# A graph network kernel: four PSUM banks for messages and two for falls in layers 1 to 3

## The chip, the cores and the metric

The kernel runs on one core of a Trainium2 chip. The metric is the device time of one execution in microseconds, and the median of several runs counts. All times in this document are microseconds unless they are marked ns.

## The reference

A graph of 3125 nodes and 100000 edges, sorted by target node, goes through four layers. Each layer gathers, for each edge, the features of its source node, adds the edge's own features, and takes a softmax-weighted mean over the edges of each target node, feature by feature. Then each node's sum goes through a small network of two linear maps with a normalisation.

```python
def _genconv(h, edge_attr, src, dst, w1, b1, g1, bb1, w2, b2, t):
    msg = jax.nn.relu(h[src] + edge_attr) + EPS_MSG
    m = msg * t
    seg_max = jax.lax.stop_gradient(jax.ops.segment_max(m, dst, num_segments=N))
    ex = jnp.exp(m - seg_max[dst])
    denom = jax.ops.segment_sum(ex, dst, num_segments=N)
    alpha = ex / (denom[dst] + 1e-16)
    agg = jax.ops.segment_sum(msg * alpha, dst, num_segments=N)
    out = h + agg
    z = jax.nn.relu(_layernorm(out @ w1 + b1, g1, bb1))
    return z @ w2 + b2
...
h = x @ enc_node_w + enc_node_b
e = edge_attr @ enc_edge_w + enc_edge_b
h = _genconv(h, e, src, dst, ...)                      # layer 0
for i in range(1, L):                                  # layers 1 to 3
    z = jax.nn.relu(_layernorm(h, ln_g[i], ln_b[i]))
    h = h + _genconv(z, e, src, dst, ...)
return jax.nn.relu(_layernorm(h, ln_g[0], ln_b[0]))
```

Before this x is normalised, and the result is added to x. There are 64 features.

## The kernel before

The edges are cut into two halves, which lie beside each other on the 128 partitions (64 features each). Each half is 98 chunks of 512 edges, so a tile is 128 x 512, which fills one PSUM bank of f32. A layer is a loop over the 98 chunks (the chunk phase), then a phase over the nodes. The five engines each run their own program in order, and semaphores tie them together; what is printed below as a loop over chunks is unrolled. Layer 0 is written out, and layers 1 to 3 are one loop.

For a chunk c of layers 1 to 3:

- GpSimd (POOL) issues 8 indirect DMAs (line L521) that gather 128 rows of `z_rows` each into `zsrc[c % 4]`. It waits for `x_mm` of chunk c - 4, which says that this buffer was read.
- TensorE (PE) writes the *falls* (L776): a tile that is 0 inside a run of edges of one target and -1e30 where a new target begins. Two matmuls. Then `add_edges` (L785), one matmul of the edge features by their weights, and `add_nodes` (L790), which transposes the gathered rows onto the same bank and signals `x_mm`.
- ScalarE (ACT) does `messages(c)`: relu to `r` (L599), times t to `u` (L601), times t back into the bank (L602).
- VectorE (DVE) does `running_max(c)`: a scan (L1100) over falls and `u` into `M`, then L1102, L1106 (the falls' bank becomes the exponent of the decay) and L1108 (the messages' bank becomes the exponent of the weight).
- ScalarE does `copy_out(c - 1)`, then `exps(c)`: the decay from the falls' bank to SBUF (L606), the exponential in the messages' bank (L608).
- VectorE does `running_sums(c)`: scan S (L1117), a product (L1119), scan W (L1121), which signals `sw_done`.
- TensorE does `back(c)`: eight transposes (L801) of S and W into the banks pT0 and pT1. ScalarE's `copy_out(c)` (L614, two of 512 columns) brings them to SBUF, and SyncE (SP) stores them to `sw_rows` (L388). SyncE's queue also loads the edge features, six pairs of chunks ahead (L380).

When all chunks are stored, GpSimd fetches the 25 groups of rows that end the nodes' runs (L532), and the node phase begins. Its result, `z_rows`, is what GpSimd waits for before the next layer's first gather. In between, the seam of the two halves is mended (L1232 to L1254).

TensorE's program sets the order of the work around the change. For chunk c it is `back(c - 3)`, `falls(c)`, `add_edges(c)`, `add_nodes(c)`, and behind the last chunk the three transposes that are left. The falls and the messages take their banks in turn from three each, so both wait for the chunk c - 3: the falls for `decay_done`, the edges for `sw_done`. VectorE's scan L1100 waits for `u_done` alone; since the falls of a chunk stand ahead of its additions, they are ready when `u` is. `banks` and `done(...)` turn a chunk into a semaphore's value (`PRE` = 2 is added to each at the start).

## Time and profile before

| | us |
|---|---|
| median of 3 runs | 4319.33 |
| lowest, highest | 4317.49, 4326.74 |
| the profiled execution | 4317.04 |
| its span | 4315.2 |

| engine | busy us | share of the span |
|---|---|---|
| GpSimd (POOL) | 3058.1 | 71% |
| VectorE (DVE) | 2874.9 | 67% |
| TensorE (PE) | 2470.6 | 57% |
| ScalarE (ACT) | 1759.0 | 41% |

The span runs from the first to the last instruction; 1.8 us of the profiled execution's time lie around it. Busy time leaves out register, branch, semaphore and DMA-issuing instructions of the engines, but a gather that GpSimd issues is shown as a span on GpSimd. "Issue" is idle time of an engine that waits for nothing that the profile shows. In the timeline, the bracket behind a row is the idle time of its engine before it, and what ended it. The mean granted clock of TensorE is 0.678 of full speed.

### The profile page before, as it was taken

Reading aid. Unit: us, or ns where it says so; the run is one execution under the profiler, and the core shown is the slowest. Engines: PE = TensorE matmul, PEld = TensorE weight load, DVE = VectorE, ACT = ScalarE, POOL = GpSimd, SP = SyncE. Lnnn points to the kernel's source line nnn. Section 1 sums busy time; section 2 is a strip of 40 time slices with the busy share of each in tenths; the row PEclk is TensorE's granted clock in tenths of the full one; section 3 lists DMA queues with packets and bytes.
Section 4 is the critical chain, followed back from the end, with each engine's and each line's share of the span. In section 5 each row is a group of like instructions: output and inputs, shape, how many; then the busy total and the mean of one; then the engine's idle time right before and its main releaser. Section 6 shows DMA issues by size and latency. Waiting matters only on the chain.

```text
span 4315.2 us, 37180 instructions
## 1 busy us (share of the span) xinstructions
PE 2470.6 (57%) x9731; PEld 1778.7 (41%) x9731; DVE 2874.9 (67%) x3973; ACT 1759.0 (41%) x3487; POOL 3058.1 (71%) x3248
## 2 busy tenths in 40 slices
PE   4666776665555555555555555555555555555554
PEld 3555555543433333333433333333343333333333
DVE  5888888875566666666656666666664666666665
ACT  2444444444433443334334433444343334443344
POOL 3777777775577777777557777777746777777773
PEclk9776667666566666666557666666656667666765
DMA  3545554554233333333223333333323333333332
GB/s 86 148 142 146 148 142 142 147 146 139 65 105 105 109 104 104 105 105 109 77 72 109 105 101 108 105 109 105 101 70 87 102 108 105 109 105 101 108 105 64
DMA packets 307125, 469.66 MB, mean 109 GB/s; under 512 B 169424, under 2 KB 175306, under 8 KB 306893
## 3 DMA queue, kind: packets, MB, share of 16 engines
q1 hardware_dynamic: 200286, 356.83, 24.0%
q0 software_dynamic: 103552, 109.52, 12.6%
q8 instruction: 86, 1.41, 0.1%
q14 instruction: 147, 1.20, 0.1%
q10 hardware_dynamic: 3054, 0.71, 0.1%
HBM read 217.93 MB, written 248.86 MB: 108 GB/s over the span
## 4 chain that ended last, share of the span: by engine, by line
POOL 69%; issue 23%; PE 2%; DVE 2%; DMA 1%; ACT 1%; POOLq 0%; ACTq 0%; DVEq 0%; SPq 0%
POOL zsrc L521 68%; POOL node_sw L532 1%; DMA zsrc<-z_rows,idx_all 1%; PE pT L801 0%; PE pR L898 0%; PE pX L790 0%; DMA node_sw<-sw_rows,row_idx 0%; PE pX L723 0%; PE pX L879 0%; DVE z L1295 0%; DMA sw_rows<-sw_out 0%; ACT sq L654 0%; ACT sw_out L614 0%; POOLq L517 0%; DMA z_rows<-z 0%
## 5 line engine op out<-in xcount | busy, mean ns | idle before, releaser
L521 POOL DMA_INDIRECT zsrc<-z_rows,idx_all x3136 | 2960.4, 944 | 1089.2 <-issue 979.3
L790 PE MATMUL pX<-ident,zsrc 128*128 128x128 f32 x2368 | 591.8, 429 | 1207.0 <-DMA zsrc<-z_rows,idx_all 1206.8
L614 ACT ACTIVATE sw_out<-pT 128x512 f32<-128x512 f32 x784 | 425.3, 594 | 1822.9 <-PE pT L801 1821.2
L790 PEld LDWEIGHTS pX<-ident,zsrc 128*128 128x128 f32 x2368 | 505.6, 316 | 1521.6 <-DMA zsrc<-z_rows,idx_all 1521.6
L1117 DVE TENSOR_TENSOR_SCAN S<-decay,S,pX 128x512 f32<-128x512 f32 x296 | 378.1, 1277 | 691.2 <-ACT decay L606 688.5
L801 PE MATMUL pT<-ident,S 128*128 128x128 f32 x1568 | 630.4, 406 | 46.2 <-DVE W L1121 46.2
L801 PE MATMUL pT<-ident,W 128*128 128x128 f32 x1568 | 619.3, 400 | 0.0
L1100 DVE TENSOR_TENSOR_SCAN M<-pR,M,u 128x512 f32<-128x512 f32 x296 | 376.8, 1273 | 235.1 <-ACT u L601 235.1
L785 PE MATMUL pX<-attr_pair,edge_w 128*128 128x512 f32 x592 | 435.4, 825 | 12.6 <-ACT attr_pair L593 12.5
L790 PE MATMUL pA<-ident,zsrc 128*128 128x128 f32 x768 | 195.0, 434 | 426.8 <-DMA zsrc<-z_rows,idx_all 426.8
L599 ACT ACTIVATE r<-pX,edge_b 128x512 f32<-128x512 f32 x296 | 204.7, 692 | 494.8 <-PE pX L790 494.8
L1121 DVE TENSOR_TENSOR_SCAN W<-decay,W,pX 128x512 f32<-128x512 f32 x296 | 378.9, 1280 | 10.4
L790 PEld LDWEIGHTS pA<-ident,zsrc 128*128 128x128 f32 x768 | 166.8, 321 | 527.4 <-DMA zsrc<-z_rows,idx_all 527.4
L801 PEld LDWEIGHTS pT<-ident,S 128*128 128x128 f32 x1568 | 358.4, 229 | 49.4 <-issue 36.4
L801 PEld LDWEIGHTS pT<-ident,W 128*128 128x128 f32 x1568 | 356.3, 227 | 0.0
L1117 DVE TENSOR_TENSOR_SCAN S<-decay,S,pA 128x512 f32<-128x512 f32 x96 | 122.9, 1280 | 320.7 <-ACT decay L606 320.7
L601 ACT ACTIVATE u<-r,t_now 128x512 f32<-128x512 f32 x392 | 283.0, 722 | 12.8
L1102 DVE TENSOR_TENSOR pR<-pR,M 128x512 f32<-128x512 f32 x296 | 207.0, 699 | 10.2
L1119 DVE TENSOR_TENSOR pX<-r,pX 128x512 f32<-128x512 f32 x296 | 205.9, 696 | 10.2
L1106 DVE TENSOR_TENSOR pR<-pR,M 128x512 f32<-128x512 f32 x296 | 207.0, 699 | 3.4
L1108 DVE TENSOR_TENSOR pX<-pX,M 128x512 f32<-128x512 f32 x296 | 203.9, 689 | 0.0
L602 ACT ACTIVATE pX<-r,t_now 128x512 f32<-128x512 f32 x296 | 199.0, 672 | 0.0
(201 smaller groups left out, 3130.9 us busy)
## 6 DMA issues: line engine op xcount, KB each, us to landing
sw_rows<-sw_out SPq DMA_DIRECT2D x392, 512.0 KB, 2.9
attr_pair<-attr_cols SPq DMA_DIRECT2D x153, 512.0 KB, 4.6
zsrc<-z_rows,idx_all POOLq DMA_INDIRECT x3136
attr_in<-in_edge_attr_dram SPq DMA_DIRECT2D x196, 128.0 KB
attr_cols<-attr_pair SPq DMA_DIRECT2D x49, 512.0 KB, 3.1
max_cols<-M SPq DMA_DIRECT2D x49, 256.0 KB, 3.1
z_rows<-z SPq DMA_DIRECT2D x25, 125.0 KB
node_sw<-sw_rows,row_idx POOLq DMA_INDIRECT x100, 2.5
```

The lines of the kernel that those rows point to most:

```text
L521: pool.indirect_dma_start(zsrc[c % RING][:, t4, h, :], None, z_rows, bass.IndirectOffsetOnAxis(idx_all[:, h, t4, c:c + 1].bitcast(U32), 0) ...
L601: act.activation(u[s][:, :], r[s][:, :], ACT.Copy, scale=t_now[:, 0:1]).then_inc(u_done, 1)
L614: act.activation(sw_out[c % 2][:, :, 2 * b:2 * b + 2, :, :].rearrange("p h t s c -> p (t s) h c"), pT[b][:, :].rearrange("p (a h c) -> p a ...
L785: pe.matmul(messages_bank(c, first_layer)[:, :], edge_w2[:, :], attr_t(c), start=True, stop=False, skip_group_check=True)
L790: last = pe.matmul(messages_bank(c, first_layer)[:, t4:CH:SUB], zsrc[c % RING][:, t4, :, :].rearrange("p h c -> p (h c)"), ident[:, :], st ...
L801: last = pe.transpose(pT[b][:, at:at + P], scanned[c % 2][:, t4:CH:SUB], ident[:, :])
L1100: v.tensor_tensor_scan(m[:, at + 1:at + CH + 1], falls[:, :], u[c % 2][:, :], m_last, ALU.add, ALU.max).then_inc(m_done, 1)
L1102: v.tensor_tensor(falls[:, :], falls[:, :], m[:, at:at + CH], ALU.add).then_inc(d_done, 1)
L1106: v.tensor_tensor(falls[:, :], falls[:, :], m[:, at + 1:at + CH + 1], ALU.subtract).then_inc(dm_done, 1)
L1117: v.tensor_tensor_scan(S[s][:, :], decay[s][:, :], msg[:, :], S[s1][:, CH - 1:CH], ALU.mult, ALU.add).then_inc(s_done, 1)
L1119: v.tensor_tensor(msg[:, :], r[s][:, :], msg[:, :], ALU.mult).then_inc(rex_done, 1)
L1121: v.tensor_tensor_scan(W[s][:, :], decay[s][:, :], msg[:, :], W[s1][:, CH - 1:CH], ALU.mult, ALU.add).then_inc(sw_done, 1)
```

## The change

In layers 1 to 3 the bank pH goes over from the falls to the messages. Messages then take four banks in turn (pX0, pX1, pA, pH), falls two (pR0, pR1), as in layer 0. The edges of chunk c wait for `sw_done` of chunk c - 4, the falls for `decay_done` of chunk c - 2. TensorE's program for chunk c becomes `back(c - 4)`, `add_edges(c)`, `add_nodes(c)`, `falls(c - 2)`, and behind the last chunk stand `back` and `falls` of what is left. Since the falls no longer stand ahead of their chunk's additions, they have a semaphore of their own, `falls_mm`, and VectorE's scan waits for it in all layers.

```diff
--- before.py
+++ after.py
@@ -232,11 +232,10 @@
 
         def messages_bank(c, first_layer):
 
-            return pX[c % 2] if first_layer else (pX + [pA])[c % 3]
-
-        def falls_bank(c, first_layer):
-
-            return pR[c % 2] if first_layer else (pR + [pH])[c % 3]
+            return pX[c % 2] if first_layer else (pX + [pA, pH])[c % 4]
+
+        def falls_bank(c):
+            return pR[c % 2]
 
         par_in = sem("par_in")
         dst_in = sem("dst_in")
@@ -264,6 +263,7 @@
         attr_tp = sem("attr_tp")
         attr_sb = sem("attr_sb")
         x_mm = sem("x_mm")
+        falls_mm = sem("falls_mm")
         r_done = sem("r_done")
         u_done = sem("u_done")
         u_ps_done = sem("u_ps_done")
@@ -603,7 +603,7 @@
 
                 def exps(c):
                     act.wait_ge(dm_done, done(g0 + c))
-                    act.activation(decay[c % 2][:, :], falls_bank(c, first_layer)[:, :], ACT.Exp).then_inc(decay_done, 1)
+                    act.activation(decay[c % 2][:, :], falls_bank(c)[:, :], ACT.Exp).then_inc(decay_done, 1)
                     act.wait_ge(um_done, done(g0 + c))
                     act.activation(messages_bank(c, first_layer)[:, :], messages_bank(c, first_layer)[:, :], ACT.Exp).then_inc(ex_done, 1)
 
@@ -738,6 +738,7 @@
 
             pe.sem_inc(attr_tp, PRE)
             pe.sem_inc(x_mm, PRE)
+            pe.sem_inc(falls_mm, PRE)
             pe.sem_inc(back_tp, PRE)
             pe.sem_inc(node_tp, PRE)
             pe.sem_inc(y_mm, PRE)
@@ -760,7 +761,7 @@
                     pe.wait_ge(z_ready, l * NG)
                     pe.sem_inc(pe_passed, 1)
 
-                banks = 2 if first_layer else 3
+                banks = 2 if first_layer else 4
 
                 def attr_to_channels(c):
                     pe.wait_ge(attr_loaded[c % 2], 32 * (c // 2 + 1))
@@ -771,10 +772,11 @@
                     last.then_inc(attr_tp, 1)
 
                 def falls(c):
-                    pe.wait_ge(decay_done, done(g0 + (c - banks)))
+                    pe.wait_ge(decay_done, done(g0 + (c - 2)))
                     for h in range(2):
-                        pe.matmul(falls_bank(c, first_layer)[h * H:(h + 1) * H, :], chunk_sel[:, c:c + 1].to_broadcast([NCH, H]), fall_sb[:, h, :],
-                                  start=True, stop=True)
+                        last = pe.matmul(falls_bank(c)[h * H:(h + 1) * H, :], chunk_sel[:, c:c + 1].to_broadcast([NCH, H]), fall_sb[:, h, :],
+                                         start=True, stop=True)
+                    last.then_inc(falls_mm, 1)
 
                 def add_edges(c):
                     if first_layer:
@@ -813,9 +815,9 @@
                 if first_layer:
                     attr_to_channels(0)
                     pe.matmul(pH[0:NP, 0:NK], zeros_b[:, :], zeros_b[:, 0:NK], start=True, stop=False, **hist_mm)
-                falls(0)
-                add_edges(0)
                 if first_layer:
+                    falls(0)
+                    add_edges(0)
                     for c in range(NCH):
                         add_nodes(c)
                         if c + 1 < NCH:
@@ -841,18 +843,18 @@
                             falls(c + 1)
                             add_edges(c + 1)
                 else:
-                    add_nodes(0)
-                    for c in range(1, 3):
-                        falls(c)
+
+                    for c in range(NCH):
+                        if c >= 4:
+                            back(c - 4)
                         add_edges(c)
                         add_nodes(c)
-                    for c in range(3, NCH):
-                        back(c - 3)
+                        if c >= 2:
+                            falls(c - 2)
+                    for c in range(NCH - 2, NCH):
+                        back(c - 2)
                         falls(c)
-                        add_edges(c)
-                        add_nodes(c)
-                    for c in range(NCH - 3, NCH - 1):
-                        back(c)
+                    back(NCH - 2)
                 back(NCH - 1)
 
                 pe.wait_ge(seam_mean, l + 1)
@@ -1086,7 +1088,7 @@
 
                 def running_max(c):
                     q, at = c // 2, (c % 2) * CH
-                    falls, msg, m = falls_bank(c, first_layer), messages_bank(c, first_layer), M[q % 2]
+                    falls, msg, m = falls_bank(c), messages_bank(c, first_layer), M[q % 2]
                     if at == 0:
                         m_last = M[(q - 1) % 2][:, 2 * CH:2 * CH + 1]
                         v.tensor_copy(m[:, 0:1], m_last)
@@ -1096,6 +1098,7 @@
                             dve.wait_ge(m_stored[q], 16 * (M_STORES[q] + 1))
                     else:
                         m_last = m[:, at:at + 1]
+                    dve.wait_ge(falls_mm, done(g0 + c))
                     dve.wait_ge(u_done, done(g0 + c))
                     v.tensor_tensor_scan(m[:, at + 1:at + CH + 1], falls[:, :], u[c % 2][:, :], m_last, ALU.add, ALU.max).then_inc(m_done, 1)
                     dve.wait_ge(m_done, done(g0 + c))
```

TensorE's program at the end of the chunk phase, from the falls or edges of chunk 97 on, before (names as in the section on the kernel; L801 is `back`, whose eight transposes are cut to the first, pR1 and pX1 are the banks of chunk 97):

```order
L776 MATMUL pR1<-fall_sb,chunk_sel 64x512 [waits decay_done]
...
L785 MATMUL pX1<-attr_pair6,edge_w2 128x512 [waits sw_done,cols_loaded6]
L790 MATMUL pX1<-ident,zsrc1 128x128 [waits gathered1]
L790 MATMUL pX1<-ident,zsrc1 128x128 x3
...
L797 REGISTER_ALU [waits sw_done]
L801 MATMUL pT0<-ident,S1 128x128 [waits back_sb]
...
L797 REGISTER_ALU [waits sw_done]
L801 MATMUL pT0<-ident,S0 128x128 [waits back_sb]
...
L797 REGISTER_ALU [waits sw_done]
L801 MATMUL pT0<-ident,S1 128x128 [waits back_sb]
```

The same place after the change (L777 is the falls, L787 the edges, L792 the nodes, L803 `back`):

```order
L787 MATMUL pX1<-attr_pair6,edge_w2 128x512 [waits sw_done,cols_loaded6]
L792 MATMUL pX1<-ident,zsrc1 128x128 [waits gathered1]
L792 MATMUL pX1<-ident,zsrc1 128x128 x3
L777 MATMUL pR1<-fall_sb,chunk_sel 64x512 [waits decay_done]
L777 MATMUL pR1<-fall_sb,chunk_sel 64x512
...
L799 REGISTER_ALU [waits sw_done]
L803 MATMUL pT0<-ident,S0 128x128 [waits back_sb]
...
L777 MATMUL pR0<-fall_sb,chunk_sel 64x512 [waits decay_done]
...
L799 REGISTER_ALU [waits sw_done]
L803 MATMUL pT0<-ident,S1 128x128 [waits back_sb]
...
L777 MATMUL pR1<-fall_sb,chunk_sel 64x512 [waits decay_done]
```

Before, the falls of chunk 97 stand ahead of its additions and three transposes (S1, S0, S1: chunks 95, 96, 97) behind them. Now the falls of chunk 95 (pR1) follow the additions of chunk 97, then come the transposes of chunk 94, the falls of 96 (pR0), the transposes of 95, and the falls of 97 (pR1). The transposes of 96 and 97 follow and are not shown.

VectorE's program for one chunk of layers 1 to 3, before (the scans are named SCALAR_TENSOR_TENSOR here):

```order
L1100 SCALAR_TENSOR_TENSOR M1<-pH,M0,u0 128x512 [waits u_done]
L1102 TENSOR_TENSOR pH<-pH,M1 128x512 [waits m_done]
L1104 COPY kept_max<-M1 128x1
L1106 TENSOR_TENSOR pH<-pH,M1 128x512 [waits d_done]
L1108 TENSOR_TENSOR pA<-pA,M1 128x512 [waits u_ps_done]
L1117 SCALAR_TENSOR_TENSOR S0<-decay0,S1,pA 128x512 [waits sw_done,back_tp,ex_done,decay_done]
L1119 TENSOR_TENSOR pA<-r0,pA 128x512 [waits s_done]
L1121 SCALAR_TENSOR_TENSOR W0<-decay0,W1,pA 128x512 [waits rex_done]
```

And after:

```order
L1103 SCALAR_TENSOR_TENSOR M1<-pR0,M0,u0 128x512 [waits u_done,falls_mm]
L1105 TENSOR_TENSOR pR0<-pR0,M1 128x512 [waits m_done]
L1107 COPY kept_max<-M1 128x1
L1109 TENSOR_TENSOR pR0<-pR0,M1 128x512 [waits d_done]
L1111 TENSOR_TENSOR pA<-pA,M1 128x512 [waits u_ps_done]
L1120 SCALAR_TENSOR_TENSOR S0<-decay0,S1,pA 128x512 [waits sw_done,back_tp,ex_done,decay_done]
L1122 TENSOR_TENSOR pA<-r0,pA 128x512 [waits s_done]
L1124 SCALAR_TENSOR_TENSOR W0<-decay0,W1,pA 128x512 [waits rex_done]
```

The instructions and their order are the same on VectorE; the scan into M waits for `falls_mm` too, and banks have changed.

## Rows read from the trace of the kernel before

**Rows 1.** The page's part 4: shares of the chain that ended last.

```profile
POOL 69%; issue 23%; PE 2%; DVE 2%; DMA 1%; ACT 1%; POOLq 0%; ACTq 0%; DVEq 0%; SPq 0%
```

**Rows 2.** GpSimd's line L521, layers 1 to 3: durations, then idle us, times.

```profile
L521 POOL DMA_INDIRECT zsrc<-z_rows,idx_all x2352: 940/944/961, 1118.5 to 4222.6; - x196
...
  issue: 741.9, 2346
  DMA z_rows<-z: 53.0, 2
  PE pX L790: 0.9, 3
  PE pA L790: 0.3, 1
```

**Rows 3.** Timeline of GpSimd: start us, us, what, idle before.

```profile
1059.86 0.94 POOL L532 DMA_INDIRECT node_sw<-sw_rows,row_idx  x1 [23.17 <-DMA sw_rows<-sw_out]
...
1118.51 0.94 POOL L521 DMA_INDIRECT zsrc<-z_rows,idx_all  x1 [25.69 <-DMA z_rows<-z]
...
2095.90 0.96 POOL L521 DMA_INDIRECT zsrc<-z_rows,idx_all  x1 [0.30 <-issue]
...
2122.14 0.94 POOL L532 DMA_INDIRECT node_sw<-sw_rows,row_idx  x1 [25.28 <-DMA sw_rows<-sw_out]
...
2182.28 0.94 POOL L521 DMA_INDIRECT zsrc<-z_rows,idx_all  x1 [27.32 <-DMA z_rows<-z]
```

**Rows 4.** Waits, layers 1 to 3: us in total, times, longest.

```profile
POOL node_sw L532 <- DMA sw_rows<-sw_out: 75.4, 3, 25.3
```

**Rows 5.** Chain that ended last, drain of layer 1: start us, us, what.

```profile
2098.38 2.08 PE pX L790 x8
2100.45 1.72 PE pT L801 x8
...
2104.41 1.29 DVE S L1117
...
2106.45 1.29 DVE W L1121
...
2112.09 1.29 DVE S L1117
...
2117.63 1.09 ACT sw_out L614 x2
2118.74 2.61 DMA sw_rows<-sw_out
```

**Rows 6.** Timeline, all engines, before and in that drain.

```profile
2092.46 0.64 PE L776 MATMUL pR<-fall_sb,chunk_sel 98*64 98x512 bf16 x2
...
2093.03 1.26 PE L785 MATMUL pX<-attr_pair,edge_w 128*128 128x512 f32 x2
...
2098.07 1.27 DVE L1100 TENSOR_TENSOR_SCAN M<-pR,M,u 128x512 f32<-128x512 f32 x1
...
2100.03 0.23 PEld L801 LDWEIGHTS pT<-ident,S 128*128 128x128 f32 x1
...
2100.72 0.69 DVE L1108 TENSOR_TENSOR pX<-pX,M 128x512 f32<-128x512 f32 x1
...
2102.25 1.09 ACT L614 ACTIVATE sw_out<-pT 128x512 f32<-128x512 f32 x2 [5.64 <-PE pT L801]
...
2103.70 0.62 ACT L608 ACTIVATE pX<-pX 128x512 f32<-128x512 f32 x1
```

**Rows 7.** Timeline of TensorE: two node additions of layer 2, closest found.

```profile
2274.76 2.08 PE L790 MATMUL pA<-ident,zsrc 128*128 128x128 f32 x8 [6.10 <-DMA zsrc<-z_rows,idx_all]
...
2283.33 1.16 PE L790 MATMUL pX<-ident,zsrc 128*128 128x128 f32 x8 [3.74 <-DMA zsrc<-z_rows,idx_all]
```

**Rows 8.** Waits in layer 0, 200 to 1000 us.

```profile
DVE M L1100 <- ACT u L601: 137.0, 76, 3.6
```

**Rows 9.** Windows: engines busy us (instructions), TensorE's clock, DMA share, GB/s.

```profile
2100.00:2108.00 8.00, 2.29 (x12) 1.90 (x11) 4.93 (x8) 3.96 (x7) 0.00 (x0) 0.50 0.16 66
```

## Prediction

> **What bounds the kernel now.** I read the chain of waits first. On the page, 69% of the chain that ended last is GpSimd and 23% is "issue", GpSimd's own gap between two gathers [rows 1]. So of every edit I ask whether it reaches GpSimd. Next I read line L521 over layers 1 to 3, from their first gather to their last: 2352 gathers of 944 ns, and the idle time before them is 741.9 us "issue" (0.30 us each, and a loop start), 53.0 us for the z rows at two layer starts, and only 0.9 + 0.3 = 1.2 us for TensorE's node additions, which is the one thing that PSUM banks can influence [rows 2]. GpSimd is never short of a free gather buffer. A chunk takes 8 x 1.248 = 9.98 us of it, and 784 gathers take from 1118.51 to 2096.86, 978 us, whatever the other engines do [rows 3].
>
> What remains of a layer is 1063.8 us (from 1118.51 to 2182.28) less 978: about 85 us in which GpSimd waits. Of it, 25.28 us lie between the last gather and the first fetch of node sums [rows 3]; over three layers this wait is 75.4 us [rows 4]. This is the drain: the last chunks run through the other engines with nothing beside them. The chain of layer 1's drain shows each link [rows 5]: node additions of chunk 97 at 2098.38 (call it T), transposes L801 of chunk 95, copy L614, decay, scan S of chunk 96 at 2104.41 (T + 6.03), W, transposes, copy, S of chunk 97 at 2112.09, transposes, copy at 2117.63, the store, then GpSimd at 2122.14. One chunk of the drain costs 2112.09 - 2104.41 = 7.68 us. Note what is already running at T: the running maximum (L1100) of chunk 96 started at 2098.07, before T [rows 6].
>
> **The change part by part.**
>
> *Four message banks instead of three.* The addition of chunk c now waits for the sums of chunk c-4, not c-3. It can only let an addition go sooner, and additions wait for the gather, with TensorE idle 3.74 to 6.10 us before them [rows 7]. Value at most the 1.2 us of [rows 2] in the whole kernel; I take 0.
>
> *The transposes go back one chunk further.* TensorE did back(c-3) ahead of the additions of chunk c; now back(c-4). ScalarE stands at copy_out(c-1), behind which are exps(c) and messages(c+1), until back(c-1) is done, so all of ScalarE's work after it, and VectorE's sums, come one chunk later against the gathers. SyncE's store of the copied rows (with the load of edge columns queued behind it, which runs six pairs ahead) comes later too. None of these holds GpSimd: its condition is the addition of chunk c-4, and a chunk landed has some three laps, 30 us, to be added. In steady state this costs nothing.
>
> *The falls two chunks behind, with a signal.* falls(c-2) now stands behind the additions of chunk c, and VectorE's running maximum of chunk c-2 waits for it. Queued behind that wait is all of VectorE's work on the chunk; ScalarE's exps wait for it, then S and W, then the transposes. So from the falls to the end of W is the new lap: by VectorE, maximum to L1108's end 3.34 us (2098.07 to 2101.41, [rows 6]), exp to S 0.70 (2103.70 to 2104.41), S to W's end 3.32 (2104.41 to 2107.73), together 7.4; by the transposes behind the falls, to the copy 2.2, copy to S 2.16 (2102.25 to 2104.41), S to W 3.32, together 7.7. The lap available is 9.98 on average and 8.57 in the shortest that I found (2274.76 to 2283.33, [rows 7]). It fits, so again nothing in steady state. In layer 0 TensorE's order is unchanged and the falls are ready a chunk ahead; VectorE's additional wait is covered by 137.0 us of waiting for u over 76 chunks [rows 8]: 0.
>
> *The drain.* Here the cover is gone. At T VectorE used to be in the middle of chunk 96's maximum; now even chunk 95's has not begun, since falls(95) stand behind the additions of chunk 97. So three chunks have to pass instead of two, one of them half done. In steps, layer 1:
> - T to the first matmul behind the additions: unchanged, 1.65 us (2098.38 to 2100.03, [rows 6]).
> - falls(95), newly ahead of the transposes: 0.57 us (2092.46 to 2093.03, [rows 6]), up to 0.9 with the gap around them. I take 0.75.
> - back(94), copy, exps, S of chunk 95: as before for back(95) to S(96), so S(95) starts at T + 6.03 + 0.75 = T + 6.8. VectorE's own path is no later: falls ready at T + 2.4, maximum 3.34, exp 0.70, T + 6.5.
> - S(95) to S(96), S(96) to S(97): 7.68 each. falls(96) stand ahead of back(95) and wait for nothing late; falls(97) stand behind back(95), done some 3 us after W(95), and the maximum of chunk 97 is wanted only after W(96).
> - S(97) therefore at T + 6.8 + 15.4 = T + 22.1, before T + 13.7. Everything behind it (last transposes, store, fetch of node sums, seam) shifts as it is.
>
> Growth per layer 0.75 + 7.68 = 8.4 us, for three layers 25.3 us. The waits of the three drains are alike (75.4 over 3, longest 25.3), so one serves for all. T itself cannot come earlier: it is 1.5 us after GpSimd's last gather ends (2096.86 to 2098.38). Bounds per layer: below, if the two cycles ran at what VectorE is busy in one plus the exp (3.32 for the sums and 3.34 for the maximum are 6.66, plus 0.70: 7.36), 0.57 + 7.68 - 2 x 0.32 = 7.6; above, if each of three chunks lost another 0.7 to the later falls and additional waits, 10.5. So 23 to 32 us in three layers. I take 25.3, since the cycle of 7.68 us is one that the trace shows whole.
>
> Sum: 4317.04 + 25.3 = 4342.3 us against the profiled execution, which lies 2.3 us under the median of 4319.33. Against the median it is 4344.6; I forecast 4344.5.
>
> TensorE's granted clock is 0.50 (1.2 GHz) in the drain, where it is busy 2.29 of 8 us [rows 9]. The transposes' durations used here are read at this level, so a drain that is longer at the same level brings no further term.
>
> **Rivals.**
>
> *A. More banks pay, and the drain does not grow.* Place: GpSimd's wait for node additions, and the first step after T. Price: 1.2 us gained at most [rows 2], so about 4318 us. It needs a drain in which chunk 95 and 96 overlap so well that each layer grows by under 2.9 us (8.6 us in all, 0.2%); from there the result is no longer slower. For it: TensorE and ScalarE are mostly idle in the drain. Against it: VectorE is busy 6.66 of each 7.68 us there, and one more whole chunk must go through it after T. The Trainium skill speaks for this rival: its page "Perfetto Trace Analysis", section "Matmuls", says that independent matmul groups should rotate through different PSUM banks, so that reading one out overlaps the next group's matmuls. By this rule alone the kernel would gain. The trace does not bear it out here: what more overlap could still free is the 1.2 us of GpSimd's waits [rows 2].
>
> *B. The lagged lap does not fit.* If falls, maximum, exps, S and W, transposes and additions ran in series, a chunk would take 1.65 + 0.57 + 3.34 + 0.70 + 3.32 + 2.2 + 1.26 (additions of edges, [rows 6]) = 13.0 us. It decides from 9.98 us on: then TensorE falls behind, GpSimd finds its four buffers full, and the kernel becomes 3.0 x 98 x 3 = 880 us longer, 5200 in all. For it: three engines in one loop, where TensorE stands in order. Against it: 7.7 us by the rows, and the transposes wait for a W of the lap before.
>
> *C. The drain is hidden.* If the fetch of node sums waited for something else than the last store, the drain would cost nothing and the time stay at 4319. Against it: the wait is put down to the store in all of the three layers, and the chain runs through it [rows 4, 5].
>
> **How the numbers follow.** Forecast 89%; A 3%; B 3%; C 3%; 2% for a GpSimd or DMA effect of unknown sign. A difference under 0.2% (8.6 us) can't be told from no change in this kernel. The growth of 23 to 32 us on the median gives 4342 to 4351; with the runs' own spread of some 2 us I give 4339 to 4352. Faster by over 0.2%: 2% (1 of A, 1 unknown). Within: 5% (2 of A, 3 of C). Slower: 93% (89 + 3 of B + 1 unknown).
>
> **What would show it.** In the profile after: gathers from first to last of a layer still 978 us; GpSimd's wait ahead of the node fetch 33 to 34 us in layers 1 to 3 and unchanged (23.17, [rows 3]) in layer 0; three S scans of the last bank cycle behind the last gathered additions, 7.7 us apart, where there were two; no wait of GpSimd for additions. The forecast is wrong if that wait is under 28 us or the gathers of a layer take over 980 us.

## The result, and the profile after

The changed kernel takes 4346.95 us (median of 4 runs, 4346.4 to 4347.7), the kernel before 4318.9 us (median of 4 runs). The ratio of the two is 1.0066 (95% interval 1.0054 to 1.0077): slower by 28 us, inside the forecast range of 4339 to 4352, and 2.5 us over the forecast of 4344.5. The profiled execution took 4346.48 us (span 4344.7), 29.4 us more than that of before.

The page of the changed kernel, parts 1, 4 and 5 (columns as for before):

```profile
PE 2503.0 (58%) x9731; PEld 1769.0 (41%) x9731; DVE 2902.7 (67%) x3973; ACT 1769.2 (41%) x3487; POOL 3057.9 (70%) x3248
...
POOL 66%; issue 22%; DMA 4%; PE 4%; DVE 2%; ACT 1%; POOLq 0%; DVEq 0%; ACTq 0%; SPq 0%
...
L521 POOL DMA_INDIRECT zsrc<-z_rows,idx_all x3136 | 2960.4, 944 | 1089.8 <-issue 968.7
L1103 DVE TENSOR_TENSOR_SCAN M<-pR,M,u 128x512 f32<-128x512 f32 x392 | 503.3, 1284 | 1009.6 <-PE pR L777 829.0
```

GpSimd still leads the chain [rows 1], with the same 2960.4 us in the gathers. The large new wait is VectorE's, 829.0 us for the falls (L777). It is idle time of an engine that does not set the pace, so by its size it says nothing of the 28 us.

GpSimd's line L521 in layers 1 to 3 of the changed kernel, which answers to [rows 2]:

```profile
L521 POOL DMA_INDIRECT zsrc<-z_rows,idx_all x2352: 938/944/962, 1117.1 to 4242.2; - x196
its engine sat idle before it (us, times) until:
  issue: 731.3, 2310
  DMA z_rows<-z: 53.4, 2
  PE pX L792: 7.0, 23
  PE pH L792: 4.3, 14
  PE pA L792: 0.9, 3
```

The waits for additions have grown from 1.2 to 12.2 us, but "issue" has shrunk by as much: 731.3 + 12.2 = 743.5, before 741.9 + 1.2 = 743.1. The longest of these waits is 0.3 us: they are the same gaps of 0.30 us under another label. A layer's gathers take 978.3 to 978.4 us, as before.

GpSimd's timeline at the drains of layers 0 to 3 and its waits there, which answer to [rows 3, 4]:

```profile
1058.42 0.94 POOL L532 DMA_INDIRECT node_sw<-sw_rows,row_idx  x1 [21.82 <-DMA sw_rows<-sw_out]
...
2131.01 0.94 POOL L532 DMA_INDIRECT node_sw<-sw_rows,row_idx  x1 [35.52 <-DMA sw_rows<-sw_out]
...
3204.53 0.94 POOL L532 DMA_INDIRECT node_sw<-sw_rows,row_idx  x1 [35.06 <-DMA sw_rows<-sw_out]
...
4278.85 0.94 POOL L532 DMA_INDIRECT node_sw<-sw_rows,row_idx  x1 [35.69 <-DMA sw_rows<-sw_out]
```

```profile
POOL node_sw L532 <- DMA sw_rows<-sw_out: 106.3, 3, 35.7
```

The wait has grown from 75.4 to 106.3 us: 30.9 us. Layer 0 gave back 1.35 us (23.17 before, 21.82 now). 30.9 - 1.35 is 29.5, which is the whole difference of the spans. So the drains of layers 1 to 3 are the place; all else cancels. Layer 0's gain was not forecast, and no run explains it (s2 lies 1.6 us under s1 there as well, f1 0.4 us over the kernel before).

The chain in the drain of layer 1, which answers to [rows 5]:

```profile
2094.53 4.28 DMA zsrc<-z_rows,idx_all
2098.85 2.08 PE pX L792 x8
2100.93 0.57 PE pR L777 x2
2101.49 1.69 PE pT L803 x8
2103.27 1.08 ACT sw_out L614 x2
...
2105.59 1.29 DVE S L1120
...
2109.05 1.99 PE pT L803 x8
...
2113.28 1.29 DVE S L1120
...
2120.97 1.29 DVE S L1120
...
2126.50 1.09 ACT sw_out L614 x2
2127.61 2.61 DMA sw_rows<-sw_out
```

Three S scans stand behind the last additions (T = 2098.85) where there were two, 7.69 us apart. S of chunk 97 starts at T + 22.12. The forecast said T + 22.1. But T itself is late: GpSimd's last gather ended at 2131.01 - 35.52 = 2095.49, so T is 3.36 us behind it, and was 1.52 us behind. In layers 2 and 3 it is 2.82 and 3.46 (before 1.47 and 1.46). Split in two, the growth of the three waits is

| | layer 1 | layer 2 | layer 3 | sum |
|---|---|---|---|---|
| last gather's end to T, longer by | 1.84 | 1.35 | 2.00 | 5.2 |
| T to the fetch of node sums, longer by | 8.40 | 8.80 | 8.45 | 25.7 |

SyncE's queue shows what meets the last gather. Before:

```profile
2083.40 0.33 SPq L388 DMA_DIRECT2D sw_rows<-sw_out  x1
2083.84 0.37 SPq L380 DMA_DIRECT2D attr_pair<-attr_cols  x1
2093.74 0.33 SPq L388 DMA_DIRECT2D sw_rows<-sw_out  x1
```

After:

```profile
2092.82 0.33 SPq L388 DMA_DIRECT2D sw_rows<-sw_out  x1
...
2093.26 0.37 SPq L380 DMA_DIRECT2D attr_pair<-attr_cols  x1
```

The layer's last load of edge columns (L380, 512 KB) stands in SyncE's program behind a store that waits for ScalarE's copy. The copy comes one chunk later now, and with it the load moved from 2083.84 (13.0 us ahead of the last gather's end) to 2093.26, 2.2 us ahead of that end at 2095.49. In layers 2 and 3 it is the same: 13.0 and 12.9 us ahead before, 1.8 and 2.2 us after.

### The profile page after: what moved, and what is told of

Its sections match the earlier page's. It is cut to its first block, busy times and chain, and to the rows that moved or that the text cites. A ratio compares the mean times of both kernels' runs of the same rounds, so it can differ in the third digit from the quotient of the medians.

```text
span 4344.7 us, 37515 instructions
## 1 busy us (share of the span) xinstructions
PE 2503.0 (58%) x9731; PEld 1769.0 (41%) x9731; DVE 2902.7 (67%) x3973; ACT 1769.2 (41%) x3487; POOL 3057.9 (70%) x3248
## 3 DMA queue, kind: packets, MB, share of 16 engines
q1 hardware_dynamic: 200286, 356.83, 23.7%
## 4 chain that ended last, share of the span: by engine, by line
POOL 66%; issue 22%; DMA 4%; PE 4%; DVE 2%; ACT 1%; POOLq 0%; DVEq 0%; ACTq 0%; SPq 0%
POOL zsrc L521 65%; DMA zsrc<-z_rows,idx_all 3%; POOL node_sw L532 1%; PE pX L792 1%; PE pT L803 1%; PE pH L792 0%; PE pR L900 0%; ACT sw_out L614 0%; PE pX L881 0%; DVE S L1120 0%; DVE W L1124 0%; PE pX L723 0%; DMA node_sw<-sw_rows,row_idx 0%; ACT sq L654 0%; DVE z L1298 0%
## 5 line engine op out<-in xcount | busy, mean ns | idle before, releaser
L521 POOL DMA_INDIRECT zsrc<-z_rows,idx_all x3136 | 2960.4, 944 | 1089.8 <-issue 968.7
L1103 DVE TENSOR_TENSOR_SCAN M<-pR,M,u 128x512 f32<-128x512 f32 x392 | 503.3, 1284 | 1009.6 <-PE pR L777 829.0
L792 PE MATMUL pX<-ident,zsrc 128*128 128x128 f32 x1984 | 474.6, 414 | 964.8 <-DMA zsrc<-z_rows,idx_all 964.8
L792 PEld LDWEIGHTS pX<-ident,zsrc 128*128 128x128 f32 x1984 | 404.6, 302 | 1258.6 <-DMA zsrc<-z_rows,idx_all 1258.6
L803 PE MATMUL pT<-ident,S 128*128 128x128 f32 x1568 | 649.2, 418 | 68.3 <-DVE W L1124 67.8
L803 PE MATMUL pT<-ident,W 128*128 128x128 f32 x1568 | 618.4, 399 | 0.0
L803 PEld LDWEIGHTS pT<-ident,S 128*128 128x128 f32 x1568 | 348.9, 222 | 196.2 <-issue 183.8
L1120 DVE TENSOR_TENSOR_SCAN S<-decay,S,pX 128x512 f32<-128x512 f32 x248 | 316.8, 1278 | 129.0 <-ACT decay L606 126.4
L787 PE MATMUL pX<-attr_pair,edge_w 128*128 128x512 f32 x496 | 379.8, 859 | 23.1 <-ACT attr_pair L593 12.1
L792 PE MATMUL pH<-ident,zsrc 128*128 128x128 f32 x576 | 149.5, 441 | 394.9 <-DMA zsrc<-z_rows,idx_all 394.9
L599 ACT ACTIVATE r<-pX,edge_b 128x512 f32<-128x512 f32 x248 | 170.9, 689 | 478.1 <-PE pX L792 478.1
L803 PEld LDWEIGHTS pT<-ident,W 128*128 128x128 f32 x1568 | 352.8, 225 | 0.0
L792 PEld LDWEIGHTS pH<-ident,zsrc 128*128 128x128 f32 x576 | 128.3, 328 | 483.6 <-DMA zsrc<-z_rows,idx_all 483.6
L1124 DVE TENSOR_TENSOR_SCAN W<-decay,W,pX 128x512 f32<-128x512 f32 x248 | 317.5, 1280 | 8.7
L1105 DVE TENSOR_TENSOR pR<-pR,M 128x512 f32<-128x512 f32 x392 | 274.1, 699 | 13.6
L792 PE MATMUL pA<-ident,zsrc 128*128 128x128 f32 x576 | 137.2, 413 | 250.4 <-DMA zsrc<-z_rows,idx_all 250.4
L1109 DVE TENSOR_TENSOR pR<-pR,M 128x512 f32<-128x512 f32 x392 | 274.1, 699 | 3.4
L606 ACT ACTIVATE decay<-pR 128x512 f32<-128x512 f32 x392 | 236.3, 603 | 93.4 <-DVE pR L1109 91.0
L792 PEld LDWEIGHTS pA<-ident,zsrc 128*128 128x128 f32 x576 | 116.6, 300 | 329.2 <-DMA zsrc<-z_rows,idx_all 329.2
L777 PE MATMUL pR<-fall_sb,chunk_sel 98*64 98x512 bf16 x784 | 235.6, 599 | 0.0
```

Source lines behind the costliest of these rows:

```text
L521: pool.indirect_dma_start(zsrc[c % RING][:, t4, h, :], None, z_rows, bass.IndirectOffsetOnAxis(idx_all[:, h, t4, c:c + 1].bitcast(U32), 0) ...
L606: act.activation(decay[c % 2][:, :], falls_bank(c)[:, :], ACT.Exp).then_inc(decay_done, 1)
L787: pe.matmul(messages_bank(c, first_layer)[:, :], edge_w2[:, :], attr_t(c), start=True, stop=False, skip_group_check=True)
L792: last = pe.matmul(messages_bank(c, first_layer)[:, t4:CH:SUB], zsrc[c % RING][:, t4, :, :].rearrange("p h c -> p (h c)"), ident[:, :], st ...
L803: last = pe.transpose(pT[b][:, at:at + P], scanned[c % 2][:, t4:CH:SUB], ident[:, :])
L1103: v.tensor_tensor_scan(m[:, at + 1:at + CH + 1], falls[:, :], u[c % 2][:, :], m_last, ALU.add, ALU.max).then_inc(m_done, 1)
```

## The experiments

Most experiments met a second condition, in which the kernel before took 5037 to 5137 us where it took 4319 in the first comparison, while the engines' instructions had their usual lengths. One of these chips (the one of e5_zero_lag) gave 4318 us for the same kernel at a later time, so this is a condition and not a property of the chip. The expectations call it "late transfers". That name is a guess, and the trace of e5 speaks against it as the whole cause. ScalarE's relu (L599) waits there for TensorE's additions (L790) and a product of VectorE that is long done, for no transfer:

```profile
1704.37 1.52 PE L790 MATMUL pX<-ident,zsrc 128*128 128x128 f32 x8
...
1707.71 0.38 PE L801 MATMUL pT<-ident,S 128*128 128x128 f32 x1 [1.82 <-DVE W L1116]
...
1714.35 0.69 ACT L599 ACTIVATE r<-pX,edge_b 128x512 f32<-128x512 f32 x1 [10.19 <-remote]
```

The additions end at 1705.89 and TensorE goes on to its transposes, but the relu starts at 1714.35, 8.5 us later; in f2, the same kernel under the first condition, it starts at 2106.46, 0.04 us behind additions that end at 2106.42. So signals between engines come late as well. What makes them late stays open, and the names of releasers in traces of this condition are not reliable.

Ratios below are against the kernel before on the same chip at that time. Three figures of each trace are compared: the length of a layer's gathers, GpSimd's wait ahead of the node fetch (the drain), and the part of the drain from the start of the last additions (T) to the fetch. The part ahead of T also holds chunks that were gathered but not yet added. The gathers' length varies by itself in the second condition: in layer 0, where TensorE's order is the same in every kernel, it was 1208 to 1266 us in the eight traces.

**e1_load_first**: the load ahead of the store.

```diff
-                for c in range(NCH):
-                    if c % 2 == 0:
-                        sp.wait_ge(x_mm, done(g0 + (c - 1)))
-                        load_cols((c // 2 + PAHEAD) % NPAIR)
+                sp.wait_ge(x_mm, done(g0 - 1))
+                load_cols(PAHEAD)
+                for c in range(1, NCH):
+                    if c % 2 and c + 1 < NCH:
+                        sp.wait_ge(x_mm, done(g0 + c))
+                        load_cols(((c + 1) // 2 + PAHEAD) % NPAIR)
                     if c >= 2:
                         store_sw(g0, c - 2)
```

> The changed kernel, with SyncE's load of edge columns issued as soon as the additions of the odd chunk before are done, ahead of the store of the copied rows instead of behind it. My theory: of the 28 us by which the change is longer, about 5 come from the last gather of each of the three layers landing late (3.36, 2.82 and 3.46 us behind the end of its issue, where it was 1.52, 1.47 and 1.46), because a load of 512 KB is now issued at 2093.26, just ahead of it, where before it was at 2083.84. Then this kernel is 5 us faster than the changed one, about 4341.5, and the additions of chunk 97 start some 1.5 us behind the last gather's issue. Rival: the late landing comes from the stores or from chance; then it stays near 4347.

Measured under the second condition: 5249.57 us, ratio 1.0225 (1.019 to 1.026); drains 55.3, 54.5 and 49.3 us. Nothing about a term of 5 us can be read from that. f1 repeats it.

**e2_back4_falls1**: falls one chunk behind instead of two.

```diff
-                        if c >= 2:
-                            falls(c - 2)
-                    for c in range(NCH - 2, NCH):
-                        back(c - 2)
-                        falls(c)
+                        if c >= 1:
+                            falls(c - 1)
+                    back(NCH - 4)
+                    falls(NCH - 1)
+                    back(NCH - 3)
                     back(NCH - 2)
```

> The changed kernel with the falls one chunk behind the additions instead of two; the transposes stay four chunks behind. My theory: a whole chunk of the drain is decided by the transposes, since ScalarE works in order and the exps of chunk c stand behind copy_out(c-1). Then the drain stays as in the changed kernel (S of the last chunk 22.1 us behind the last additions' start) and the time at 4347 within 2 us. Rival: the falls' place and their signal decide; then half of the growth or all of it goes, 4320 to 4333.

Measured under the second condition: 5186.83 us, ratio 1.0098 (1.006 to 1.0136). Drains 46.9, 54.4 and 54.2 us; the changed kernel's under this condition (c1, on another chip) are 50.1, 53.9 and 54.2. From T to the fetch 34.0, 33.9 and 35.1 us, in c1 33.4, 33.9 and 33.8. Layer 2's last additions and fetch:

```profile
3819.64 1.29 PE L792 MATMUL pX<-ident,zsrc 128*128 128x128 f32 x8
...
3853.49 0.95 POOL L532 DMA_INDIRECT node_sw<-sw_rows,row_idx  x1 [54.39 <-DMA sw_rows<-sw_out]
```

The drain is that of the changed kernel, as the theory says: with the falls alone a chunk nearer, nothing of it goes. The absolute time was forecast for the first condition and can't be tested.

**e3_back3_falls1**: four banks and two, falls one chunk behind, transposes three chunks behind as before.

```diff
-                        if c >= 4:
-                            back(c - 4)
+                        if c >= 3:
+                            back(c - 3)
                         add_edges(c)
                         add_nodes(c)
-                        if c >= 2:
-                            falls(c - 2)
+                        if c >= 1:
+                            falls(c - 1)
...
```

> The changed kernel (four banks for messages, two for falls) with the falls one chunk behind and the transposes three chunks behind as before. My theory: the chunk of 7.68 us is gone, and only the falls ahead of the first transposes of the drain stay: 0.75 us in each layer, so about 4321.5 (2 us over the kernel before). Rival, the falls' place decides: halfway, about 4333 or more.

Measured under the second condition: 5217.91 us, ratio 1.0151 (1.0118 to 1.0184). Drains 41.8, 47.2 and 41.4 us. From T to the fetch 26.2, 26.5 and 27.0 us, on average 7.8 less than in e2 on the same chip, which is one lap: the additional chunk is gone. Layer 2:

```profile
3859.73 1.92 PE L792 MATMUL pX<-ident,zsrc 128*128 128x128 f32 x8
...
3886.23 0.94 POOL L532 DMA_INDIRECT node_sw<-sw_rows,row_idx  x1 [47.22 <-DMA sw_rows<-sw_out]
```

The kernel is still slower than before, and 31 us slower than e2, whose range it does not touch. Its three drains are 25 us shorter than e2's, but its gathers take 1143 to 1146 us in layers 1 to 3 where e2 has 1116 to 1129, 61 us more in all.

**e4_banks_only**: TensorE's order of before, with four banks and two.

```diff
-                        if c >= 4:
-                            back(c - 4)
+                        if c >= 3:
+                            back(c - 3)
+                        falls(c)
                         add_edges(c)
                         add_nodes(c)
-                        if c >= 2:
-                            falls(c - 2)
...
```

> Banks alone: four for messages and two for falls, TensorE in the order of before (transposes of c-3, falls of c, edges of c, nodes of c). The falls now wait in TensorE for the decay of chunk c-2, which by the rows of before is 3.8 us behind the start of the transposes; with the edges that makes 7.3 us from one chunk's additions, under the shortest lap seen of 8.6. My theory: no cost and no gain, 4319 within 2 us, gathers of a layer still 978 us. Rival: four banks pay by themselves, under 4315; or that wait holds the additions back, over 4325.

Measured under the second condition: 5162.03 us, ratio 1.0059 (1.0036 to 1.0081). Drains 46.5, 42.3 and 42.4, of which T to the fetch 23.2, 23.7 and 24.4, as in the kernel before; gathers 1121 to 1123 us. Four banks by themselves pay nothing there. Whether they are free under the first condition was not measured.

**c1_after_again** and **c2_before_traced**: the changed kernel and the kernel before, unaltered, on one chip.

> The changed kernel unaltered. The experiments so far met two chips on which the kernel before takes 5120 to 5140 us instead of 4319, with engine instructions of unchanged length but transfers that report their end later. There GpSimd no longer sets the pace alone. If this chip is like those: my theory is that the change costs more there than its 28 us, because its additional chunk of drain is longer (a lap of some 12 us against 7.7, three times) and the store of the copied rows, which ScalarE waits for, comes later: 5165 to 5200. Rival: with late transfers the fourth bank pays, and the change is even or faster. On a chip like the first: 1.0066 of the kernel before.

> The kernel before unaltered, for its trace on the same chip as the changed kernel. If transfers report late here, GpSimd's gathers of a layer take more than 978 us and ScalarE's copies wait for stores (an unknown releaser) rather than for transposes; if not, the trace is that of the first chip.

Measured under the second condition: changed 5177.48 us against 5050.65, ratio 1.0209 (1.0145 to 1.0273). The kernel before took 5064.01 us in the one execution of c2, which is its trace. Timelines of GpSimd, layer 2's fetch of node sums, before and changed:

```profile
3760.44 0.94 POOL L532 DMA_INDIRECT node_sw<-sw_rows,row_idx  x1 [37.20 <-DMA sw_rows<-sw_out]
```

```profile
3848.23 0.94 POOL L532 DMA_INDIRECT node_sw<-sw_rows,row_idx  x1 [53.92 <-DMA sw_rows<-sw_out]
```

A wait of the kernel before under this condition (in total, times, longest):

```profile
ACT sw_out L614 <- remote: 1749.1, 165, 49.8
```

"Remote" is a releaser that the profile can't name. GpSimd no longer sets the pace by itself (487.5 us of its own waits end with "remote", though its program waits for TensorE alone between two chunks), and the change costs more: drains 39.2, 37.2 and 38.7 us before, 50.1, 53.9 and 54.2 changed (43 us in all), gathers of layers 1 to 3 1108 to 1112 against 1132 to 1137 us (71 us in all), and 15 us in layer 0's gathers, where TensorE's order is the same; so how much of the 71 us is the change's is not shown.

The time lies in the range of the theory, but by luck: the kernel before took 5051 us here, not 5120 to 5140, so the change cost 127 us, more than the theory had. And a lap of some 12 us in the drain is not what the traces show: from T on the S scans of the changed kernel are 7.2 to 7.7 us apart, and T to the fetch costs 24 us more in three layers (33.4, 33.9 and 33.8 against 25.5, 26.4 and 25.0), as under the first condition. The other 19 of the 43 us lie ahead of T: the changed kernel had more chunks left to add when the last gather ended.

**e5_zero_lag**: the kernel before with no more lag than needed.

```diff
-                    add_nodes(0)
-                    for c in range(1, 3):
-                        falls(c)
-                        add_edges(c)
-                        add_nodes(c)
-                    for c in range(3, NCH):
-                        back(c - 3)
-                        falls(c)
-                        add_edges(c)
-                        add_nodes(c)
-                    for c in range(NCH - 3, NCH - 1):
-                        back(c)
+                    for c in range(NCH):
+                        add_nodes(c)
+                        if c >= 1:
+                            back(c - 1)
+                        if c + 1 < NCH:
+                            falls(c + 1)
+                            add_edges(c + 1)
```

> The kernel before (three banks for messages and three for falls) with TensorE's order of layer 0 in layers 1 to 3: the additions of chunk c, the transposes of chunk c-1, the falls and edges of chunk c+1. Nothing lags behind the gathers more than it must. My theory, the drain is chunks of lag: behind the last gathered additions of a layer at T, ScalarE makes r and u (to T + 3.5), the maximum takes 3.34, exp 0.70, the sums 3.32, so the last W ends at about T + 11 where it was T + 17.0; 6 us less in each of three layers, about 4301 on a chip where the kernel before takes 4319 (0.4% faster). A chunk's latency, 11 us from its additions to W, is less than a lap and the additions, 9.98 + 1.65, so the transposes don't wait. Rival: they do wait, and with no lag left each late gather shows; then the gathers of a layer take more than 978 us and the kernel is not faster.

Measured under the second condition: 5202.19 us, ratio 1.016 (1.0086 to 1.0234). Drains 35.2, 35.8 and 41.2 us (T to the fetch 17.7, 19.4 and 19.2), the shortest of all under this condition, but gathers of 1144 to 1150 us. The rival's outcome came: longer gathers and no faster kernel. That a missing lag lets each late signal through is the likely reason, but it is argued: no trace of the kernel before exists from this chip at that time.

**e6_serial_lap**: the transposes one chunk nearer, the falls left two behind (also in what follows the loop).

```diff
-                        if c >= 4:
-                            back(c - 4)
+                        if c >= 3:
+                            back(c - 3)
...
```

> The changed kernel (falls two chunks behind the additions) with the transposes three chunks behind instead of four: back(c-3) then stands right behind falls(c-3) of the lap before in TensorE's order, and waits for the W that these falls begin. This makes the lap of rival B real: falls, maximum, exp, S and W, transposes, edges and nodes in series. My theory: on any chip the lap becomes the sum of the rows, 13.0 us, so the 98 chunks of a layer take some 1270 us instead of 978, GpSimd waits for additions in every chunk, and the kernel takes 5200 us or more (on a chip with late transfers, where the lap is 11.5 to 12 us already, 5300 to 5700). Rival: engines overlap even here and the lap stays at 9.98 (or at what the chip allows); then my price for rival B was wrong.

Measured under the second condition, one run of each kernel: 5659.03 us against 5037.33. GpSimd's line L521 in layers 1 to 3, and a lap of TensorE:

```profile
  PE pX L792: 469.3, 135
  PE pA L792: 230.0, 66
  PE pH L792: 194.5, 63
```

```profile
1702.85 0.48 PE L803 MATMUL pT<-ident,S 128*128 128x128 f32 x1 [7.56 <-DVE W L1124]
...
1708.17 0.64 PE L777 MATMUL pR<-fall_sb,chunk_sel 98*64 98x512 bf16 x2
...
1708.86 1.28 DVE L1103 TENSOR_TENSOR_SCAN M<-pR,M,u 128x512 f32<-128x512 f32 x1 [6.09 <-PE pR L777]
```

The gathers of layers 1 to 3 take 1273.4, 1273.2 and 1272.7 us, 12.99 us a chunk, where the rows of before gave 13.0. TensorE stands 7.56 us before the transposes for the W that its own falls began, and GpSimd now waits 894 us for additions. This is the cost of rival B once the order makes it real, and that the changed kernel has none of it is due to the transposes' fourth chunk of lag.

The drains of this run are the longest of all, 77.2, 76.1 and 76.1 us. Four chunks are still to be added when the last gather ends, one every 13 us, so 39.4 to 40.4 us pass before T. From T to the fetch it is still 36.7 to 36.8 us, with three S scans 10.1 us apart, though the transposes are three chunks behind as in the kernel before:

```profile
2693.07 1.91 PE L792 MATMUL pX<-ident,zsrc 128*128 128x128 f32 x8
...
2699.65 1.28 DVE L1120 TENSOR_TENSOR_SCAN S<-decay,S,pH 128x512 f32<-128x512 f32 x1 [0.70 <-ACT decay L606]
...
2709.75 1.28 DVE L1120 TENSOR_TENSOR_SCAN S<-decay,S,pX 128x512 f32<-128x512 f32 x1 [0.70 <-ACT decay L606]
```

So the falls' place holds the additional chunk, too: with falls two chunks behind, chunk 95's maximum has not begun at T, wherever the transposes stand.

**s1_before_4out** and **s2_after_4out**: four buffers for ScalarE's copies in either kernel (the other places follow this one).

```diff
-        sw_out = two("sw_out", [P, 2, SUB, 2, H])
+        sw_out = [sb(f"sw_out{s}", [P, 2, SUB, 2, H]) for s in range(4)]
...
-                    act.wait_ge(sw_stored[c % 2], q0 * 16 + (c // 2 + 1) * 16)
+                    act.wait_ge(sw_stored[c % 4], stored_before[c % 4 // 2] + (c // 4 + 1) * 16)
```

> The kernel before with four sw_out buffers and four store semaphores instead of two; nothing else. On chips with late transfers a layer's gathers take 1110 us, since ScalarE's copy of chunk c waits for the store of chunk c-2 (1749 us of waiting for an unknown releaser at L614). My theory: with the store of chunk c-4 to wait for, a late store is covered, the gathers of a layer go down towards 978 us, and the kernel takes 4500 to 4750 where the kernel before takes 5040 to 5140; on a chip like the first it stays at 4319. Rival: the late transfers are gathers, and the wait at L614 only shows what the gathers make; then it stays within 1% of the kernel before.

> The changed kernel with the same four sw_out buffers. On a chip with late transfers the change costs 127 us: 14 to 15 us more drain and 24 us more gathers per layer, and the rest in layer 0. My theory: the longer gathers come from stores that are issued later against ScalarE's need and go away with the buffers, while the drain's additional chunk stays; the difference to s1_before_4out is then 30 to 50 us. Rival: the difference stays above 100 us, since the lag in the order, not the store, costs there. On a chip like the first, 28 us over the kernel before.

Both met the first condition. s1: 4319.32 us, ratio 1.0003 (0.9993 to 1.0012). s2: 4348.28 us, ratio 1.007 (1.0053 to 1.0087), drains 35.6, 34.2 and 35.7 us. So the buffers matter nothing here, and the change's cost stands again, in a later comparison and with another buffer count: T to the fetch is 32.4 us in each layer, and T is 3.2, 1.9 and 3.2 us behind the last gather's end, with the load issued 2.1, 3.0 and 2.0 us ahead of that end. The theory on late stores was for the second condition and stays untested.

**f1_load_first**: e1 under the first condition.

> The changed kernel with SyncE's load of edge columns issued right behind the additions of the odd chunk before, ahead of the store instead of behind it, asked for again on a chip like the first. My theory: 5 of the 28 us of the change are the last gathers' late landing beside such a load; the time is about 4342 (5 us under the changed kernel), GpSimd's wait ahead of the node fetch in layers 1 to 3 some 33.5 us instead of 35.4, and the additions of chunk 97 start 1.5 us behind the end of the last gather's issue. Rival: the landing stays late (2.8 us and more) and the time at 4347.

Measured: 4351.47 us, ratio 1.0058 (1.0044 to 1.0071). On this chip the kernel before lay at 4318.6 us in one run and at 4325.4 to 4327.4 in eight, and f1 at 4344.35 in one (the profiled one) and at 4350.0 to 4352.6 in four. Level against level it is 25 to 26 us over the kernel before, where the changed kernel is 28 us over it: a gain of 2 to 3 us, not the 5 of the theory. SyncE's queue and the last additions of layer 2:

```profile
3158.51 0.37 SPq L380 DMA_DIRECT2D attr_pair<-attr_cols  x1
3169.77 8.41 SPq L388 DMA_DIRECT2D sw_rows<-sw_out  x2
```

```profile
3172.75 1.41 PE L794 MATMUL pX<-ident,zsrc 128*128 128x128 f32 x8 [2.50 <-DMA zsrc<-z_rows,idx_all]
...
3204.32 0.94 POOL L534 DMA_INDIRECT node_sw<-sw_rows,row_idx  x1 [33.90 <-DMA sw_rows<-sw_out]
```

The load is away from the last gather. The additions start 2.08, 2.33 and 1.58 us behind its end (sum 6.0; changed kernel 9.6, before 4.4), and the drains are 34.3, 33.9 and 33.3 us, 4.7 less in all. So the load carries most of the late landing, 3.6 of 5.2 us. A store still starts beside the last gather, 1.4, 0.7 and 2.1 us ahead of its end in layers 1 to 3, where it was 3.0 to 3.1 us in the kernel before. The nearer the store, the later the additions (2.08, 2.33 and 1.58 us, before 1.46 to 1.52), so the rest goes with the store; no run moved the store alone. The 1.1 us left of the 4.7 lie between T and the fetch. The span gains 2.2 us, less than the drains, since layer 0's wait, unchanged in code, was 23.5 us here and 21.8 there. By the ratios alone the gain is not clear, since their intervals overlap.

**f2_zero_lag**: e5 under the first condition.

> The kernel before in TensorE's order of layer 0 (additions of c, transposes of c-1, falls and edges of c+1) in all layers, asked for again on a chip like the first. On a chip with late transfers it was 1.6% longer than before, with gathers of 1144 to 1150 us a layer. My theory for a chip like the first: gathers stay at 978 us, the last W ends 11 us behind the last additions' start where it was 17.0, GpSimd's wait ahead of the node fetch is 19 to 20 us where it was 25.1, and the kernel takes about 4301. Rival: some of it is lost to transfers that now meet the last gather (landing up to 2 us later a layer): 4307; or the gathers take longer here too.

Measured: 4308.5 us (4307.65 to 4309.59), ratio 0.9958 (0.9945 to 0.9972). The drain of layer 1, in the chain and GpSimd's timeline, and GpSimd's line:

```profile
2104.34 2.09 PE pX L790 x8
...
2114.03 1.29 DVE W L1116
```

```profile
2122.04 0.95 POOL L532 DMA_INDIRECT node_sw<-sw_rows,row_idx  x1 [19.18 <-DMA sw_rows<-sw_out]
```

```profile
L521 POOL DMA_INDIRECT zsrc<-z_rows,idx_all x2352: 943/947/962, 1122.5 to 4221.9; - x196
```

The last W ends at T + 10.98, forecast T + 11. The three waits sum to 57.6 us where [rows 4] has 75.4: 17.8 us less, forecast 18. But one gather takes 947 ns where it took 944, which makes 980.4 us of each layer's 978.4 (981.7 of 979.7 in layer 0), 7.9 us in all, and the waits for z rows are 2 us longer. By the profiles the kernel gains 7.4 us of span (4307.8 against 4315.2). The timed ratio says 18 us, with a kernel before that ran at the higher of its two levels on this chip in most runs; against its one run at the lower level, 4318.56, it is 10 us. So the gain is 0.2 to 0.4%. The forecast drain came, the forecast time of 4301 did not: the rival's "the gathers take longer here too" holds. It is the fastest kernel of the case under the first condition, and 1.6% slower than the kernel before under the second.

Split at T, the drains of layers 1 to 3 in all traces are (us; "ahead" means that a chunk's falls are written ahead of its additions):

| run | transposes, falls behind the additions by chunks | last gather's end to T | T to the fetch |
|---|---|---|---|
| *first condition* | | | |
| before, s1 | 3, ahead | 1.5 to 1.6 | 23.4 to 24.0 |
| after, s2 | 4, 2 | 1.9 to 3.5 | 32.2 to 32.4 |
| f1 | 4, 2 | 1.6 to 2.3 | 31.6 to 32.2 |
| f2 | 1, ahead | 1.5 to 1.6 | 17.7 |
| *second condition* | | | |
| c2, e4 | 3, ahead | 10.8 to 23.3 | 23.2 to 26.4 |
| c1, e1 | 4, 2 | 15.6 to 21.8 | 33.4 to 33.9 |
| e2 | 4, 1 | 12.9 to 20.5 | 33.9 to 35.1 |
| e3 | 3, 1 | 14.4 to 20.7 | 26.2 to 27.0 |
| e5 | 1, ahead | 16.4 to 22.1 | 17.7 to 19.4 |
| e6 | 3, 2 | 39.4 to 40.4 | 36.7 to 36.8 |

## Why the prediction was right

- *GpSimd sets the pace and the banks can free 1.2 us at most.* Right: gathers take 978.4 us a layer before and after. The change as a whole brought nothing (s2 against s1); the banks alone were tried in e4 only, under the second condition, and brought nothing there.
- *The transposes' lag costs nothing in steady state.* Right under the first condition. Under the second the gathers of layers 1 to 3 were 24 us longer each in c1 than in c2; whether a lag, the stores or the condition's own variation does that is open.
- *The lap is 7.7 us and fits in 9.98.* Right, and e6 shows what it costs when it does not fit: put in series, the same durations gave 12.99 us a chunk.
- *The drain grows by 0.75 + 7.68 = 8.4 us a layer.* From T on right: S of chunk 97 at T + 22.12, and 8.40, 8.80 and 8.45 us more to the fetch. The transposes start 2.64 us behind T (2101.49), where 1.65 + 0.75 = 2.4 was forecast.
- *What the chunk hangs on.* The prediction had the transposes' place make ScalarE a chunk late, and the falls' place keep chunk 95's maximum from beginning. The runs set them apart by the time from T to the fetch. With the falls alone a chunk nearer the chunk stays (e2, 34 us), with the transposes alone a chunk nearer it stays as well (e6, 37 us, in a longer lap), with both nearer it is gone (e3, 26 to 27 us, where c2 has 25 to 26). So both reasons hold, each by itself. These runs are of the second condition; under the first only the two ends (before and after) and f2 were measured, with 23.8, 32.2 and 17.7 us in layer 1.
- *T can't come earlier.* True, but it was the wrong bound: T came later, by 5.2 us in three layers. The sign "33 to 34 us" for GpSimd's wait was missed for this reason (35.1 to 35.7). The prediction named the load queued behind the store on SyncE and stopped at "none of these holds GpSimd"; it did not ask what the load meets when it starts. This is the 5 us by which the drains exceed the 25.3 of the sum, and f1 took 3.6 of them away by moving the load. Layer 0's 1.35 us, forecast as unchanged, brought the total back to 29.5. That the time still lies in the range is in part luck: a drain grew by 10.2 to 10.5 us, and the upper bound of 10.5 had been made for another loss, the falls' and waits' 0.7 us a chunk, which did not come.
- *Rival A*: nothing was gained, as the waits for additions that more banks could shorten were 1.2 us in all. For it the prediction had named the Trainium skill, whose page "Perfetto Trace Analysis", section "Matmuls", advises to rotate independent matmul groups through different PSUM banks; three banks rotated already, and a fourth with more lag cost 28 us. *Rival C*: the drain is not hidden.

## What to carry to other kernels

Where one engine sets the pace, a lag between it and its consumers is free in steady state and paid in full each time the pipeline drains: count the chunks still to pass when the last input lands, times the lap of the consumers, times the number of drains. Slack in the order can be spent the other way, too: shortening the lag took 17.8 us out of the drains here, but under the second condition the same order was 1.6% slower than the kernel before, and one chunk less lag made e3 31 us slower than e2. So measure an order under both conditions before it is kept. A transfer that is queued behind a delayed one is delayed with it, so ask what it now runs beside.

## What the runs showed of the hardware

- The same kernel on the same chip took 5121 us at one time and 4318 us at a later one. In traces under the slower condition the gathers of layers 1 to 3 took longer by over 100 us each, with the engines' instructions unchanged (a scan 1280 ns, a gather's span on GpSimd 944 to 947 ns), and waits ended late: in e5 ScalarE went on 8.5 us behind the TensorE instruction that it waited for, in f2, the same kernel, 0.04 us behind it. In the drains, where no gathers run beside, the S scans followed each other in 7.2 to 7.7 us in c1 and c2 too. A schedule's ranking depended on the condition: e5's order was 1.6% slower than before in one and 0.2 to 0.4% faster in the other.
- The last gather of a layer was added 1.5 us behind its end with the load of 512 KB issued 13 us ahead of that end, and 1.9 to 3.5 us behind it with the load issued 1.8 to 3.0 us ahead (the changed kernel and s2).
- One gather's span on GpSimd was 944 ns in the kernel before, the changed one and f1, and 947 ns in f2, with the same arguments; over 784 gathers this is 2 us a layer. Under the second condition e1, the same kernel as f1, had 947 ns too. The runs do not show why.
